# Attention of a gated cross-attention and expert layer: split products against whole fp32 operands

## The chip, the cores and the metric

The kernel is one program on one core of a Trainium2 chip. The metric is the device time of one execution in microseconds (us), the median of three runs. An execution takes about 2.16 ms.

## The reference, cut to what matters

The layer has two halves: a cross-attention from 32 batches of 256 tokens (256 features) to 77 context rows plus one null row, 16 heads of 64, and a mixture of 32 experts of which each token takes 8, with a shared expert. Each half is added to its input through a gate.

```python
q = split_heads(x @ Wq)                         # x: (32, 256, 256), layer-normalised
k, v = split(context @ Wkv)                     # context: (32, 77, 512)
k = concat(null_kv[0], k); v = concat(null_kv[1], v)      # 78 rows a head
attn = softmax(q * 64 ** -0.5 @ k.T)            # (32, 16, 256, 78)
out = layernorm((attn @ v) @ Wout)
x = x + tanh(g_xattn) * out
# then: router logits, top 8 of 32, weighted sum of the experts' gated MLPs, shared expert
x = x + tanh(g_ffn) * ffn(layernorm(x))
```

## The kernel before

The kernel has three stages. The context phase (`context_phase`, to about 242 us) multiplies the context by `Wkv` in four groups of eight batches and stores keys and values to DRAM. The attention phase (`attention_phase`) runs one step a batch, b from -2 to 33. The expert phase (`expert_phase`) works through 159 pages of 512 routed rows and 16 dense rounds; its first dense rounds run between the last attention steps.

**Split products.** A tile that enters a product is kept as two tiles of type fp32r, a high part and a low part. ACT copies a result out of PSUM into the high tile (`high`, L932), DVE subtracts that from PSUM into the low tile (`low`, L1170), and `split_product` (L138) issues three products: high by high, low by high, high by low.

**One attention step.** PE follows a written order, `RING` (L92): X transposes the normalised tokens of the batch after, N2 those of an earlier batch for the router, Oa and Ob are the output projection of the batch before, T0a to T3b transpose the probabilities, L and R are the router's logits and ranks, Q0 to Q3 the queries of the next batch, PV0a to PV1b the products of probabilities and values. Every name has one of four PSUM banks (`BANK`, L94), and PE waits in `free` (L1303) until the bank's holder before has been read. The scores of a batch are four units (two token tiles, two halves of the heads), made by `similarity` (L1282) at the start of a step (units 0 and 1) and after Oa (2 and 3): per unit four pairs of heads, each a product of 156 columns, two heads side by side in a key tile `kT` whose other halves are zero. So a step has 16 x 3 = 48 score products.

DVE takes the negated maximum of a unit (L1026), ACT the exponentials (L921), DVE normalises (L1031). The normalised probabilities are written in two pieces: 64 columns of each head (`main`), and the remaining 14 of eight heads together (`rest`, 112 columns). PE transposes `main` two heads at a time (T0a, T1a, T2a, T3a: four transposes each) and `rest` in T1b and T3b (two each): 20 transposes a step. A value product takes two heads' `main` rows, with the values on a block diagonal (`v_main`), and adds a second product with the `rest` rows (`v_rest`); 8 pairs x 2 x 3 = 48 products of 256 columns a step.

**Order on the other engines.** ACT and DVE run through `EVICTED` in PE's order, with the exponentials, normalisations, maxima and router operations hung in behind certain names (L983 to L1010, L1241 to L1268). POOL computes the two inverse deviations of a step (`make_rstd`, L833) and issues 16 indirect scatters a step of 128 rows to their pages from step 3 on (`scatter`, L844); the scatters and the statistics stand in one order (L857 to L906), and the first scatter of a step waits until the page fills of the steps before have landed. DVE's second statistics of a step stand behind the low part of T3b (L1250), and POOL's second `make_rstd` waits for them. Router product R uses Ob's bank, which `centre` (L1057) frees, and `centre` waits for POOL's first `make_rstd`.

**SP's queue.** One queue (L737 to L794) issues, step by step: the tokens two batches ahead, page fills, the values of the next batch (18 loads: two of `v_main`, eight heads of `v_rest` with two parts each), the keys of the next batch (four loads, L671), and stores. At the start come 16 loads that place the null value row (L760).

In the context phase ACT evicts each product into a high tile (L364 to L378), DVE subtracts the low part (L429 to L438), and both parts are stored; a high and a low key array and a values array of twice the width lie in DRAM.

## Time and profile before

| what | value |
|---|---|
| median of 3 runs | 2156.69 us (2154.57 to 2160.22) |
| span of the profiled execution | 2156.4 us |
| PE busy | 2034.8 us (94%) |
| DVE busy | 1768.4 us (82%) |
| ACT busy | 1387.1 us (64%) |
| POOL busy | 1204.5 us (56%) |
| DMA packets, under 512 B of them | 442777, 204984 |

The page gives the profiled execution's span, from its first to its last instruction; it has no other time for that execution. Busy time counts an engine as busy while any record of it runs. PE's records overlap, so a PE that is busy is not a PE at its peak: distances between the starts of records tell its pace. In a row of the order in time the columns are start in us, length in us, engine, line, operation, output and inputs, form, and, in brackets, the idle time before it with what ended it; "x4" is four instructions merged. PEld is PE's weight load, SPq and POOLq are the issue of DMAs by those engines. Shares over the whole span mix the three stages, so windows by stage come first.

### The profile page before, as it was taken

To read this page: it belongs to the slowest core of one execution; us is meant where nothing else is said; L and a number is where in the kernel's file an instruction comes from. 1 tells how busy PE (TensorE), PEld (TensorE's weight loads), DVE (VectorE), ACT (ScalarE), POOL (GpSimd) and SP (SyncE) were. 2 spreads that over 40 slices of the span, in tenths; PEclk is the share of its full clock that TensorE was granted. 3 is DMA by queue.
4 is the path that set the end of the run, shared out by engine and by line. 5 is a ranking of instruction groups with operands and counts; after the bars stand their busy time and mean duration, and the time that the engine had idled before them with its cause. 6 is when DMAs were issued, how large, how long until landed. Compare 5 with 4: busy or idle time off the path is not lost. (4 is left out here: it accounts for less than half of the span.)

```text
span 2156.4 us, 43812 instructions
## 1 busy us (share of the span) xinstructions
PE 2034.8 (94%) x14306; PEld 1884.7 (87%) x14306; DVE 1768.4 (82%) x4190; ACT 1387.1 (64%) x4030; POOL 1204.5 (56%) x1324
## 2 busy tenths in 40 slices
PE   7999689999999999999997889999999999999995
PEld 7888589999999999999997778988988888888884
DVE  4544258899999999999997766668999999999996
ACT  3322357677777777777774347777777777777771
POOL 0000202777777777777777600006777777777775
PEclk9999889999999999999998899999999999999997
DMA  9876489988888888788886999999999999999997
GB/s 275 280 242 216 140 240 297 304 262 249 246 252 252 252 249 250 248 249 246 248 259 224 298 360 286 287 285 365 403 403 402 397 397 395 391 392 399 393 366 280
DMA packets 442777, 645.86 MB, mean 300 GB/s; under 512 B 204984, under 2 KB 317337, under 8 KB 440089
## 3 DMA queue, kind: packets, MB, share of 16 engines
q1 hardware_dynamic: 393400, 508.79, 71.0%
q0 software_dynamic: 49152, 134.28, 17.2%
q8 instruction: 116, 1.90, 0.4%
q14 instruction: 109, 0.88, 0.1%
HBM read 325.18 MB, written 317.72 MB: 298 GB/s over the span
## 5 line engine op out<-in xcount | busy, mean ns | idle before, releaser
L1710 POOL DMA_INDIRECT parts<-results_dram,kept_index x512 | 516.1, 1008 | 382.7 <-DMA results_dram<-y 219.0
L848 POOL DMA_INDIRECT pages_dram<-rows,kept_index x512 | 509.4, 995 | 167.0 <-issue 139.1
L927 ACT ACTIVATE exps<-sim,minus_max 128x78 f32<-128x78 f32 x1024 | 320.8, 365 | 50.5 <-DVE minus_max L1028 49.9
L927 ACT ACTIVATION_READ_ACCUMULATOR exps<-sim,minus_max 128x1 f32 x1024 | 252.3, 247 | 0.0
L1731 ACT ACTIVATE w_h<-w_raw 128x768 fp32r<-128x768 f32 x159 | 134.0, 843 | 149.7 <-DMA w_raw<-in_experts 149.7
L1819 DVE SCALAR_TENSOR_TENSOR parts<-parts,kept_weight 128x256 f32<-128x256 f32 x448 | 213.6, 477 | 1.8 <-DMA parts<-dense_dram 0.7
L1916 PE MATMUL xps<-ident,xin 128*128 128x128 f32 x1272 | 167.0, 275 | 18.1 <-DVE wq_l L1781 7.9
L1793 DVE TENSOR_TENSOR w_l<-w_raw,w_h 128x768 fp32r<-128x768 f32 x159 | 151.7, 954 | 38.6 <-ACT w_h L1731 38.4
L140 PE MATMUL yps<-w_h,hid_h 128*128 128x256 f32 x636 | 180.0, 283 | 0.7 <-DVE hid_l L1876 0.7
L142 PE MATMUL yps<-w_l,hid_h 128*128 128x256 f32 x636 | 178.7, 281 | 0.0
L141 PE MATMUL yps<-w_h,hid_l 128*128 128x256 f32 x636 | 178.2, 280 | 0.0
L1738 ACT ACTIVATE y<-yps 128x512 f32<-128x512 f32 x318 | 171.8, 597 | 1.5 <-PE yps L142 1.5
L1916 PEld LDWEIGHTS xps<-ident,xin 128*128 128x128 f32 x1272 | 141.0, 141 | 26.1 <-issue 24.2
L140 PE MATMUL ring<-xnT_h,wq_h 128*128 128x256 f32 x512 | 157.7, 308 | 2.0 <-DVE xnT_l L1175 1.4
L1762 ACT ACTIVATE hid_h<-up_ps 128x512 fp32r<-128x512 f32 x175 | 103.4, 591 | 85.5 <-DVE up_ps L1870 85.0
L1781 DVE TENSOR_TENSOR wq_l<-xps,wq_h 128x512 fp32r<-128x512 f32 x212 | 143.0, 686 | 18.5 <-ACT wq_h L1725 18.5
L140 PE MATMUL sim<-kT_h,qT_h 128*128 128x156 f32 x512 | 140.9, 275 | 11.9 <-issue 7.7
L1870 DVE SCALAR_TENSOR_TENSOR up_ps<-up_ps,w_raw,act_gate 128x512 f32<-128x512 f32 x159 | 120.0, 755 | 38.0 <-PE up_ps L142 36.6
L140 PE MATMUL ring<-wo_h,outT_h 128*128 128x256 f32 x512 | 148.7, 290 | 0.2 <-DVE outT_l L1175 0.2
L141 PE MATMUL ring<-xnT_h,wq_l 128*128 128x256 f32 x512 | 145.6, 284 | 0.0
L142 PE MATMUL ring<-xnT_l,wq_h 128*128 128x256 f32 x512 | 145.3, 284 | 0.0
L141 PE MATMUL ring<-wo_h,outT_l 128*128 128x256 f32 x512 | 143.5, 280 | 0.0
(270 smaller groups left out, 7206.5 us busy)
## 6 DMA issues: line engine op xcount, KB each, us to landing
xin<-pages_dram SPq DMA_DIRECT2D x159, 512.0 KB, 10.5
results_dram<-y SPq DMA_DIRECT2D x159, 512.0 KB, 9.6
w_raw<-in_experts SPq DMA_DIRECT2D x159, 385.0 KB, 9.5
pages_dram<-blank SPq DMA_DIRECT2D x108, 512.0 KB, 4.0
pages_dram<-blank SPq DMA_DIRECT2D x12, 1536.0 KB, 8.2
values_dram<-values SPq DMA_DIRECT2D x16, 1024.0 KB
v_main<-values_dram SPq DMA_DIRECT2D x64, 256.0 KB
keys_h_dram<-keys_h SPq DMA_DIRECT2D x16, 616.0 KB, 4.8
```

Source lines behind the costliest of these rows:

```text
L140: eng.matmul(out, left[0], right[0], start=start, stop=False)
L141: eng.matmul(out, left[1], right[0], start=False, stop=False)
L142: return eng.matmul(out, left[0], right[1], start=False, stop=stop)
L848: pool.indirect_dma_start(dram["pages"], bass.IndirectOffsetOnAxis(ap=kept_index[:, at:at + 1].bitcast(U32), axis=0), buffer(batch)[:, k / ...
L927: last = act.activation(exps[u % 2][:, h, :], scores(u)[:, h // 4, h % 4, :], ACT.Exp, bias=minus_max[u][:, h:h + 1], accum_out=row_sum[u] ...
L1710: pool.indirect_dma_start(parts[slot(batch, t)][:, k, :], None, done, bass.IndirectOffsetOnAxis(ap=kept_index[:, at:at + 1].bitcast(U32), ...
L1731: act.activation(w_split[s][0][:, :], w_raw[s][:, 0:EW], ACT.Copy).then_inc(w_hi, 1)
L1738: last = act.activation(y[s][:, q:q + 2, :], yps[:, q:q + 2, :], ACT.Copy)
L1781: dve.tensor_tensor(xT[m % XT][1][:, c, :], xps[:, c, :], xT[m % XT][0][:, c, :].bitcast(F32), ALU.subtract).then_inc(x_lo, 1)
L1793: dve.tensor_tensor(w_split[s][1][:, :], w_raw[s][:, 0:EW], w_split[s][0][:, :].bitcast(F32), ALU.subtract).then_inc(w_lo, 1)
L1819: dve.scalar_tensor_tensor(out=out, in0=part[:, k, :], scalar=kept.weight[:, at:at + 1], in1=part[:, TOPK, :], op0=ALU.mult, op1=ALU.add). ...
L1916: last = pe.transpose(xps[:, c, q * P:(q + 1) * P], xin[s][:, q, c * P:(c + 1) * P], ident[:, :])
```

## The change

Attention works on whole fp32 operands instead of split ones.

- *Scores.* `qT` and `kT` become single fp32 tiles; a pair of heads is one fp32 product of 156 columns, 16 a step instead of 48. The queries have no low part.
- *Transposes.* The probabilities of a head stay together, 78 columns; each head is transposed by itself, 32 transposes a step in eight names (T0a, T0b, ... T3b), and ACT evicts 78 partitions of 512 columns into one fp32 tile `pT`. There is no low part.
- *Values.* `v` is one tile of 78 rows by 16 heads by 64. A value product takes one head: 64 columns of weights, 256 columns of `pT`. The even head of a pair writes PSUM partitions 0 to 63, the odd one 64 to 127. 16 products a step instead of 48.
- *Waits.* Only X, N2 and the value results still have low parts (`SPLIT`); users of the others wait for ACT alone. The second statistics still stand behind T3b, whose low part is skipped. `RING` and `BANK` are rewritten: T0a and T0b, T1a and T1b, T2a and T2b, T3a and T3b are neighbours, and the banks go round in another order.
- *Context phase.* DVE alone copies keys and values out of PSUM, ACT does nothing for them; DVE waits for the stores. Keys and values are stored once, half the bytes.
- *DMA.* Per step one load of values instead of 18, two of keys instead of four. The null value row is loaded by two DMAs at the start of SP's queue instead of being split and placed by 16. POOL no longer clears value tiles.

```diff
...
-RING = ["X", "N2", "Oa", "T0a", "Ob", "T1a", "L", "Q0", "T1b", "Q1", "PV0a", "PV0b", "T2a", "R", "T3a", "Q2", "T3b", "Q3",
-        "PV1a", "PV1b"]
-BANK = {"X": 1, "N2": 2, "Oa": 3, "T0a": 0, "Ob": 3, "T1a": 1, "L": 2, "Q0": 0, "T1b": 1, "Q1": 2, "PV0a": 1, "PV0b": 0, "R": 3,
-        "T2a": 2, "T3a": 1, "Q2": 0, "T3b": 3, "Q3": 2, "PV1a": 1, "PV1b": 0}
+RING = ["X", "N2", "Oa", "T0a", "T0b", "Ob", "T1a", "T1b", "L", "Q0", "Q1", "PV0a", "PV0b", "T2a", "T2b", "R", "T3a", "T3b", "Q2",
+        "Q3", "PV1a", "PV1b"]
+BANK = {"X": 2, "N2": 0, "Oa": 3, "T0a": 1, "T0b": 2, "Ob": 3, "T1a": 0, "T1b": 1, "L": 2, "Q0": 0, "Q1": 1, "PV0a": 2, "PV0b": 0,
+        "T2a": 1, "T2b": 2, "R": 3, "T3a": 0, "T3b": 1, "Q2": 2, "Q3": 3, "PV1a": 0, "PV1b": 1}
 NBANK = 4
 EVICTED = [n for n in RING if n[0] not in "OLR"]
+SPLIT = [n for n in EVICTED if n in ("X", "N2") or n[0] == "P"]
...
-ROUTE_AFTER = {"T1a": ["logits", "top", "mask"], "PV0b": ["placed"], "Q3": ["opened", "page", "moved", "slot"],
+ROUTE_AFTER = {"T1b": ["logits", "top", "mask"], "PV0b": ["placed"], "Q3": ["opened", "page", "moved", "slot"],
...
-                        for out, tile in zip(keys_out, keys[unit % KSLOTS]):
-                            sp.dma_start(out[:, g * CG + i * CBATCHES:g * CG + (i + 1) * CBATCHES, first:first + KPART * M],
-                                         tile[:, :, :, :].rearrange("p b q m -> p b (q m)").bitcast(F32)).then_inc(keys_stored[unit % KSLOTS], 16)
+                        sp.dma_start(keys_out[:, g * CG + i * CBATCHES:g * CG + (i + 1) * CBATCHES, first:first + KPART * M],
+                                     keys[unit % KSLOTS][:, :, :, :].rearrange("p b q m -> p b (q m)")).then_inc(keys_stored[unit % KSLOTS], 16)
...
-                    act.wait_ge(full, at(PRODUCTS, name, g))
-                    ps = bank(name)
-                    if name[0] == "K":
-                        pair, unit = int(name[2]), key_unit(name, g)
-                        if pair % KPART == 0 and unit >= KSLOTS:
-                            act.wait_ge(keys_stored[unit % KSLOTS], 32 * (unit // KSLOTS))
-                        last = act.activation(keys[unit % KSLOTS][0][:, :, pair % KPART, :],
-                                              ps[:, 0:CCOLS].rearrange("p (b m) -> p b m", m=M), ACT.Copy)
-                    else:
-                        t, half, unit = int(name[1]), int(name[2]), value_unit(name, g)
-                        if half == 0 and unit >= VSLOTS:
-                            act.wait_ge(values_stored[unit % VSLOTS], 16 * (unit // VSLOTS))
-                        last = act.activation(values[unit % VSLOTS][0:size(t), 0, half * 512:(half + 1) * 512],
-                                              ps[0:size(t), :], ACT.Copy)
-                    signal(last)
+                    skip()
...
+                    dve.wait_ge(full, at(PRODUCTS, name, g))
                     ps = bank(name)
                     if name[0] == "K":
-                        high, low = (tile[:, :, int(name[2]) % KPART, :] for tile in keys[key_unit(name, g) % KSLOTS])
-                        last = dve.tensor_tensor(low, ps[:, 0:CCOLS].rearrange("p (b m) -> p b m", m=M), high.bitcast(F32),
-                                                 ALU.subtract)
+                        pair, unit = int(name[2]), key_unit(name, g)
+                        if pair % KPART == 0 and unit >= KSLOTS:
+                            dve.wait_ge(keys_stored[unit % KSLOTS], 16 * (unit // KSLOTS))
+                        last = dve.tensor_copy(keys[unit % KSLOTS][:, :, pair % KPART, :], ps[:, 0:CCOLS].rearrange("p (b m) -> p b m", m=M))
                     else:
-                        t, half = int(name[1]), int(name[2])
-                        high, low = (values[value_unit(name, g) % VSLOTS][0:size(t), part, half * 512:(half + 1) * 512] for part in range(2))
-                        last = dve.tensor_tensor(low, ps[0:size(t), :], high.bitcast(F32), ALU.subtract)
+                        t, half, unit = int(name[1]), int(name[2]), value_unit(name, g)
+                        if half == 0 and unit >= VSLOTS:
+                            dve.wait_ge(values_stored[unit % VSLOTS], 16 * (unit // VSLOTS))
+                        last = dve.tensor_copy(values[unit % VSLOTS][0:size(t), half * 512:(half + 1) * 512], ps[0:size(t), :])
...
-    kT = [sb(f"kT_{s}", [P, PAIRS, 2 * J], F32R) for s in "hl"]
-    v_main = [sb(f"v_main{i}", [P, 2, PAIRS, P], F32R) for i in range(2)]
-    v_rest = [sb(f"v_rest{i}", [P, 2, 2, HP, P], F32R) for i in range(2)]
-    qT = [sb(f"qT_{s}", [P, PAIRS, N], F32R) for s in "hl"]
+    kT = sb("kT", [P, PAIRS, 2 * J])
+    v = [sb(f"v{i}", [J, HEADS, DH]) for i in range(2)]
+    qT = sb("qT", [P, PAIRS, N])
     exps = [sb(f"exps{i}", [P, PAIRS, J]) for i in range(2)]
-    probs = [sb(f"probs{i}", [P, PAIRS * J]) for i in range(2)]
-    pT = [sb(f"pT_{s}", [P, HP + 1, N], F32R) for s in "hl"]
+    probs = [sb(f"probs{i}", [P, PAIRS, J]) for i in range(2)]
+    pT = sb("pT", [J, PAIRS, N])
...
-        if name in ("T1b", "T3b"):
-            return ps[0:PAIRS * REST, 0:N], [t[0:PAIRS * REST, HP, :] for t in pT]
         if name[0] == "T":
-            tt = int(name[1]) % 2
-            return ps[:, :].rearrange("p (h n) -> p h n", h=4), [t[:, 0:HP, tt * P:(tt + 1) * P] for t in pT]
+            tt, h = int(name[1]) % 2, HP * "ab".index(name[2])
+            return ps[0:J, :].rearrange("p (h n) -> p h n", h=HP), [pT[:, h:h + HP, tt * P:(tt + 1) * P]]
         if name[0] == "Q":
             q = 2 * int(name[1])
-            return by_two, [t[:, q:q + 2, :] for t in qT]
+            return by_two, [qT[:, q:q + 2, :]]
...
-            for part, name in zip(kT, ("keys_h", "keys_l")):
-                of_batch = dram[name][batch].rearrange("p (q m) -> p q m", m=M)
-                for half, col in halves:
-                    sp.dma_start(part[half, :, col:col + M].bitcast(F32), of_batch[half, :, :]).then_inc(keys_loaded, 16)
+            of_batch = dram["keys"][batch].rearrange("p (q m) -> p q m", m=M)
+            for half, col in halves:
+                sp.dma_start(kT[half, :, col:col + M], of_batch[half, :, :]).then_inc(keys_loaded, 16)
 
         def load_values(batch):
 
-            of_batch = dram["values"][batch * M:(batch + 1) * M, :]
-            by_pair = of_batch.rearrange("m (a s d) -> m a s d", s=2, d=DH)
-            by_head = of_batch.rearrange("m (a h d) -> m a h d", h=PAIRS, d=DH)
-            main = v_main[batch % 2][:, :, :, :].rearrange("p s q d -> p (s q) d")
-            rest = v_rest[batch % 2][:, :, :, :, :].rearrange("p s f q d -> p (s f) q d")
-            for s in range(2):
-                sp.dma_start(main[s * DH:(s + 1) * DH, :, s * DH:(s + 1) * DH].bitcast(F32),
-                             by_pair[0:DH, :, s, :]).then_inc(values_loaded[batch % 2], 16)
-            for head in range(PAIRS):
-                col = head % 2 * DH
-                sp.dma_start(rest[head * REST:(head + 1) * REST - 1, :, head // 2, col:col + DH].bitcast(F32),
-                             by_head[DH:M, :, head, :]).then_inc(values_loaded[batch % 2], 16)
+            sp.dma_start(v[batch % 2][0:M, :, :].rearrange("m h d -> m (h d)"),
+                         dram["values"][batch * M:(batch + 1) * M, :]).then_inc(values_loaded[batch % 2], 16)
...
-        sp.dma_start(null_v[:, :], dram["null_kv"][1:2, :]).then_inc(null_loaded, 16)
+        for values in v:
+            sp.dma_start(values[M:J, :, :], dram["null_kv"][1:2, :].unsqueeze(1).broadcast_to([1, HEADS, DH])).then_inc(null_v_loaded, 16)
...
-                if b == -1:
-                    sp.wait_ge(zeroed, 1)
-                elif b >= 1:
+                if b >= 1:
...
-                if name == "T0a" and here:
+                if name == "T0b" and here:
                     exp(3, b, 0, PAIRS // 2)
-                if name == "T1a" and here:
+                if name == "T1b" and here:
...
-                dve.wait_ge(ring_full, nth(RING, "T1b" if before_u < 2 else "T3b", before_b))
-            e, inv = exps[u % 2], row_inv[u][:, :].unsqueeze(2)
-            main = probs[u % 2][:, 0:PAIRS * DH].rearrange("p (h j) -> p h j", j=DH)
-            rest = probs[u % 2][:, PAIRS * DH:PAIRS * J].rearrange("p (h j) -> p h j", j=REST)
-            dve.tensor_tensor(main, e[:, :, 0:DH], inv.broadcast_to([P, PAIRS, DH]), ALU.mult)
-            dve.tensor_tensor(rest, e[:, :, DH:J], inv.broadcast_to([P, PAIRS, REST]), ALU.mult).then_inc(probs_ready, 1)
+                dve.wait_ge(ring_full, nth(RING, f"T{before_u}b", before_b))
+            dve.tensor_tensor(probs[u % 2][:, :, :], exps[u % 2][:, :, :], row_inv[u][:, :].unsqueeze(2).broadcast_to([P, PAIRS, J]),
+                              ALU.mult).then_inc(probs_ready, 1)
...
-            if not runs(name, b):
+            if name not in SPLIT or not runs(name, b):
...
-                if name == "T1b" and here:
+                if name == "T1a" and here:
...
-            pe.wait_ge(ring_lo, nth(EVICTED, "Q3", b - 1))
-            pe.wait_ge(keys_loaded, 64 * (b + 1))
+            pe.wait_ge(ring_hi, nth(EVICTED, "Q3", b - 1))
+            pe.wait_ge(keys_loaded, 32 * (b + 1))
             if n == 0:
                 pe.wait_ge(keys_zeroed, 1)
-                pe.wait_ge(null_k_lo, 1)
+                pe.wait_ge(null_k_set, 1)
             if n >= 2:
                 pe.wait_ge(exp_done, n - 1)
             tt, half = u % 2, u // 2
             for i in range(HP):
                 pair = half * HP + i
-                last = split_product(pe, sim[u % 2][:, i // 2, (i % 2) * 2 * J:(i % 2 + 1) * 2 * J],
-                                     [t[:, pair, tt * P:(tt + 1) * P] for t in qT], [t[:, pair, :] for t in kT])
+                last = pe.matmul(sim[u % 2][:, i // 2, (i % 2) * 2 * J:(i % 2 + 1) * 2 * J], qT[:, pair, tt * P:(tt + 1) * P],
+                                 kT[:, pair, :], start=True, stop=True)
...
-                        pe.wait_ge(ring_lo, nth(EVICTED, held, at))
+                        pe.wait_ge(ring_lo if held in SPLIT else ring_hi, nth(EVICTED, held, at))
...
-            elif name in ("T1b", "T3b"):
-                first = int(name[1]) - 1
-                pe.wait_ge(probs_ready, UNITS * b + first + 2)
-                for tt in range(TT):
-                    last = pe.transpose(ps[0:PAIRS * REST, tt * P:(tt + 1) * P], probs[tt][:, PAIRS * DH:PAIRS * J], ident[:, :])
             elif name[0] == "T":
-                u = int(name[1])
+                u, first = int(name[1]), HP * "ab".index(name[2])
                 pe.wait_ge(probs_ready, UNITS * b + u + 1)
                 for i in range(HP):
-                    last = pe.transpose(ps[:, i * P:(i + 1) * P], probs[u % 2][:, i * P:(i + 1) * P], ident[:, :])
+                    last = pe.transpose(ps[0:J, i * P:(i + 1) * P], probs[u % 2][:, first + i, :], ident[:, :])
...
-                pe.wait_ge(values_loaded[par], 16 * (2 + PAIRS) * (h + 1))
+                pe.wait_ge(values_loaded[par], 16 * (h + 1))
                 if b == 0:
-                    pe.wait_ge(null_placed, 32 * PAIRS)
-                pairs = [2 * "ab".index(name[3]) + i for i in range(2)]
-                pe.wait_ge(ring_lo, nth(EVICTED, f"T{2 * half + 1}a", b))
-                for i, pair in enumerate(pairs):
-                    split_product(pe, ps[:, i * N:(i + 1) * N], [main_values(b, part, HP * half + pair) for part in range(2)],
-                                  [t[:, pair, :] for t in pT], start=i == 0, stop=False)
-                pe.wait_ge(ring_lo, nth(EVICTED, f"T{2 * half + 1}b", b))
-                for i, pair in enumerate(pairs):
-                    last = split_product(pe, ps[:, i * N:(i + 1) * N], [rest_values(b, part, half, pair) for part in range(2)],
-                                         [t[0:PAIRS * REST, HP, :] for t in pT], start=False, stop=i == 1)
+                    pe.wait_ge(null_v_loaded, 32)
+                pe.wait_ge(ring_hi, nth(EVICTED, f"T{2 * half + 1}b", b))
+                first = HP * "ab".index(name[3])
+                for i in range(2):
+                    for rows_of, _ in halves:
+                        head = first + 2 * i + (rows_of.start > 0)
+                        last = pe.matmul(ps[rows_of, i * N:(i + 1) * N], v[par][:, PAIRS * half + head, :], pT[:, head, :], start=True, stop=True)
...
```

## Rows read from the trace of the kernel before

**Rows 1.** Windows: length, busy (count) of PE, PEld, DVE, ACT, POOL; clock, DMA, GB/s

```profile
259.40:295.20 35.80, 24.86 (x168) 23.51 (x169) 16.48 (x33) 19.11 (x85) 0.00 (x0) 0.79 0.55 142
354.20:390.20 36.00, 30.21 (x234) 29.57 (x235) 28.30 (x77) 19.95 (x85) 17.67 (x21) 0.91 0.98 333
692.40:719.85 27.45, 27.32 (x235) 26.81 (x234) 25.97 (x80) 20.39 (x85) 20.62 (x24) 1.00 0.82 249
```

**Rows 2.** PE in time order: first score product of steps 1 and 31

```profile
295.23 0.47 PE L140 MATMUL sim<-kT_h,qT_h 128*128 128x156 f32 x1 [7.08 <-issue]
...
1132.19 0.24 PE L140 MATMUL sim<-kT_h,qT_h 128*128 128x156 f32 x1
```

**Rows 3.** PE in time order: transposes, then value and score products

```profile
701.32 0.61 PE L1343 MATMUL ring<-ident,probs 128*128 128x128 f32 x4
701.68 0.37 PE L140 MATMUL ring<-wo_h,outT_h 128*128 128x256 f32 x1
701.89 0.28 PE L141 MATMUL ring<-wo_h,outT_l 128*128 128x256 f32 x1
...
716.98 0.28 PE L140 MATMUL ring<-pT_h,v_main 128*128 128x256 f32 x1
...
719.85 0.24 PE L140 MATMUL sim<-kT_h,qT_h 128*128 128x156 f32 x1
719.92 0.28 PE L141 MATMUL sim<-kT_h,qT_l 128*128 128x156 f32 x1
...
720.48 0.28 PE L140 MATMUL sim<-kT_h,qT_h 128*128 128x156 f32 x1
```

**Rows 4.** POOL in time order, one step: scatters, wait for the statistics

```profile
692.54 1.07 POOL L848 DMA_INDIRECT pages_dram<-rows,kept_index  x1 [0.29 <-issue]
...
718.19 0.19 POOL L835 TENSOR_TENSOR var_eps<-mean_var,eps_col 128x2 f32<-128x2 f32 x1 [1.91 <-DVE mean_var L1053]
...
719.99 1.07 POOL L848 DMA_INDIRECT pages_dram<-rows,kept_index  x1 [0.30 <-issue]
```

**Rows 5.** Waits (us, times, longest): steps in 540 to 977, then context phase

```profile
POOL var_eps L835 <- DVE mean_var L1053: 30.5, 16, 1.9
...
ACT values L376 <- DMA values_dram<-values: 17.8, 5, 9.9
```

**Rows 6.** SP's queue in time order, during step 0

```profile
261.38 9.84 SPq L763 DMA_DIRECT2D v_rest<-null_rows  x16
...
285.96 2.02 SPq L674 DMA_DIRECT2D kT_h<-keys_h_dram  x2
```

**Rows 7.** POOL in time order, first scatter of step 3

```profile
365.48 1.24 POOL L848 DMA_INDIRECT pages_dram<-rows,kept_index  x1 [12.18 <-DMA pages_dram<-blank]
```

**Rows 8.** PE in time order, products of 512 columns in the expert phase

```profile
1319.72 0.39 PE L141 MATMUL gate_ps<-wq_h,w_l 128*128 128x512 f32 x1
...
1322.05 0.39 PE L142 MATMUL up_ps<-wq_l,w_h 128*128 128x512 f32 x1
```

**Rows 9.** Groups in 540:977.6: count, busy us, mean ns, idle before

```profile
L1175 DVE TENSOR_TENSOR pT_l<-ring,pT_h 128x512 fp32r<-128x512 f32 x64 | 44.0, 687 | 1.1
L1175 DVE TENSOR_TENSOR qT_l<-ring,qT_h 128x512 fp32r<-128x512 f32 x64 | 43.5, 679 | 4.0 <-ACT qT_h L939 4.0
L1175 DVE TENSOR_TENSOR outT_l<-ring,outT_h 128x512 fp32r<-128x512 f32 x64 | 42.1, 678 | 0.0
L939 ACT ACTIVATE pT_h<-ring 128x512 fp32r<-128x512 f32 x63 | 39.3, 625 | 7.4 <-PE ring L1343 7.4
L1069 DVE SCALAR_TENSOR_TENSOR x<-z,rstd,x 128x256 f32<-128x256 f32 x32 | 14.0, 478 | 0.0
L1061 DVE SCALAR_TENSOR_TENSOR z<-ring,mean_var,scale_row 128x256 f32<-128x256 f32 x32 | 13.9, 476 | 0.0
L1049 DVE BATCH_NORM_STATS2 stats<-x 128x6 f32<-128x256 f32 x32 | 11.9, 414 | 0.0
```

**Rows 10.** PE's weight loads in time order, one of a score product

```profile
720.19 0.19 PEld L141 LDWEIGHTS sim<-kT_h,qT_l 128*128 128x128 f32 x1
```

More of the change, by code:

```diff
@@ L186, in context_phase @@
     ctxT = [sb(f"ctxT_{s}", [P, CC, CROWS], F32R) for s in "hl"]
-    keys = [[sb(f"keys{i}_{s}", [P, CBATCHES, KPART, M], F32R) for s in "hl"] for i in range(KSLOTS)]
-    values = [sb(f"values{i}", [P, 2, INNER], F32R) for i in range(VSLOTS)]
+    keys = [sb(f"keys{i}", [P, CBATCHES, KPART, M]) for i in range(KSLOTS)]
+    values = [sb(f"values{i}", [P, INNER]) for i in range(VSLOTS)]
     banks = [ctx.enter_context(nc.psum_tensor(f"bank{i}", [P, 512], F32)) for i in range(CBANK)]
@@ L223, in staged @@
         return s.rearrange("p (c n) -> p c n", c=shape[1]) if len(shape) == 3 else s
-    keys_out = [dram[f"keys_{s}"].rearrange("b p f -> p b f") for s in "hl"]
+    keys_out = dram["keys"].rearrange("b p f -> p b f")
     def size(t):
@@ L628, in null_keys @@
         return [null_k[half, 0:1].broadcast_to([DH, PAIRS]) for half, _ in halves]
-    def main_values(batch, part, pair):
-        return v_main[batch % 2][:, part, pair, :]
-    def rest_values(batch, part, half, pair):
-        return v_rest[batch % 2][0:PAIRS * REST, part, half, pair, :]
     def buffer(batch):
@@ L805, in gpsimd @@
         pool.wait_ge(made, 3)
-        for part in kT:
-            for (half, _), (_, col) in zip(halves, reversed(halves)):
-                last = pool.memset(part[half, :, col:col + J].bitcast(F32), 0.0)
+        for (half, _), (_, col) in zip(halves, reversed(halves)):
+            last = pool.memset(kT[half, :, col:col + J], 0.0)
         last.then_inc(keys_zeroed, 1)
@@ L967, in step @@
             if b == -2:
-                act.wait_ge(null_loaded, 16)
-                act.activation(null_rows[:, 0, :, :], null_v[:, :].unsqueeze(1).broadcast_to([1, 2, DH]), ACT.Copy).then_inc(null_hi, 1)
                 act.wait_ge(null_k_loaded, 32)
                 for (half, col), null in zip(halves, null_keys()):
-                    last = act.activation(kT[0][half, :, col + M], null, ACT.Copy)
-                last.then_inc(null_k_hi, 1)
+                    last = act.activation(kT[half, :, col + M], null, ACT.Copy)
+                last.then_inc(null_k_set, 1)
             if b == 0:
```

40 lines of the change are left out of this document (8 added, 32 removed).

## The prediction, made before the changed kernel was run

> **What bounds the kernel now.** I read the windows by stage first [rows 1]. From 390 us on the attention steps repeat, and in one of them PE is busy 27.32 of 27.45 us at full granted clock (1.00), DVE 25.97, ACT 20.39 and POOL 20.62. The step starts, in PE's order of time, give the period: from step 16 to step 31, (1132.19 - 719.85) / 15 = 27.49 us [rows 2, 3]. So PE sets the step, and what a step costs is the sum of the distances between starts of its products, not the length of their records: records of 0.28 us start 0.11 to 0.12 us apart [rows 3].
>
> The next thing to read is who comes second. POOL looks three quarters busy, but its order of time [rows 4] shows scatters of about 1.0 us, sixteen a step, with 0.30 us of issue before each, and in a whole step (692.54 to 719.99, 27.45 us) it waits for another engine only once: 1.91 us for DVE's second statistics. In 16 steps that wait is 30.5 us [rows 5], 1.91 each. Hence POOL by itself needs 27.45 - 1.91 = 25.54 us a step. A faster PE meets that floor after less than 2 us.
>
> The four first steps are longer: 259.4 to 390.2, 130.8 us for four [rows 1]. Step 0 ends in a stall, 7.08 us before step 1's first score product [rows 2], and the granted clock of step 0's window is 0.79 (part of it at 1.2 GHz, the lower of the two levels). SP's order shows why: 16 loads of the null row take 9.84 us, values behind them, and the keys of step 1 are only issued at 285.96 [rows 6]. Step 3 is long because POOL's first scatter waits 12.18 us for the page fills [rows 7], which stand in the same SP queue.
>
> **The change, part by part**, against the profiled span of 2156.4 us (the median of the three runs, 2156.69, is 0.3 above it; I treat them as one).
>
> *Score products.* 48 of 156 columns become 16 whole fp32 ones. Before: 719.92 to 720.48 is five distances, 0.112 us each [rows 3], so 48 x 0.112 = 5.38 us a step. The trace has no whole fp32 product except transposes. Its floor is one of the present ones, 0.112; its ceiling follows from the kernel's own split, which treats an operand as a high and a low part: a product of two whole operands is at most four such products with a load each, 0.448. Between them lies four passes in which the loads stay hidden: 512-column products start 0.233 us apart (ten distances from 1319.72 to 1322.05, [rows 8]), 0.455 ns a column, so 4 x 156 columns take 0.284 us. I take that, because in rows 3 and 8 a load never shows where the columns take longer than it. 16 x 0.284 = 4.54: -0.84 us. The Trainium skill, "FP8 and Floating Point Precision", TensorE Precision Notes, puts a true fp32 product at four passes; by it the sum is this middle value, and no run here shows it yet.
>
> *Value products.* Before, 24 in 716.98 to 719.85, 0.1196 each [rows 3], 48 x 0.1196 = 5.74 us. After, 16 products of 256 columns and 64 output rows, alternately in the two column halves: 4 x 256 x 0.455 ns = 0.466 us each, 7.45 us one after another, 3.73 us if the halves run side by side. Floor 0.06 each (one pass, side by side), ceiling 4 x 0.1196 = 0.478. I take side by side, since the two products share neither weights, columns nor output rows: -2.01 us. No row of before shows two products in different halves, so this is the weakest step.
>
> *Entering and leaving the half-width form.* Twice a step, four edges. The nearest row is the change from transposes to products: 701.68 to 701.89, 0.21 instead of 0.11 [rows 3], 0.10 an edge, +0.40 us. If PE empties at each edge, a record less its distance is added, 0.28 - 0.12 = 0.16 more, and the sum below ends some 18 us higher. The Trainium skill, "TensorEngine Tiling (Array Packing)", Key Properties, states such a drain; rows 3 show a smaller cost for a change of kind of another sort, so they decide neither way.
>
> *Transposes.* 20 a step become 32. Four take 0.36 us from their first start to the next group's (701.32 to 701.68, [rows 3]), 0.09 each. With 78 columns to load instead of 128, 0.055 to 0.09; at 0.07, 32 x 0.07 - 20 x 0.09 = +0.44 us (-0.04 to +1.08).
>
> *PE's step* is then 27.49 - 0.84 - 2.01 + 0.40 + 0.44 = 25.48 us, a hair under POOL's 25.54. The ends of all bounds together put PE between 19 and 33 us; below 25.5 the floor is POOL's.
>
> *DVE and ACT.* DVE loses the low parts of the transposes (44.0 us in 15.9 steps, and a shorter tile beside) and of the queries (43.5), over 5.5 us a step [rows 9], and one of two products in each normalisation: from 26 to about 20 us busy. ACT evicts eight transposed tiles instead of six, at most 8 x 0.625 against 4 x 0.625 and two shorter ones [rows 9], under +2.5 us, to less than 23 of 25.5. Neither binds. Transposes and queries are free after ACT alone, so PE's waits on them end earlier.
>
> *Where POOL's wait goes.* It waits because the second statistics stand in DVE's order behind the low part of T3b. That low part is gone, so from rstd to the statistics there remain centre (2 x 0.476), two low parts of outT (2 x 0.678), the residual (2 x 0.478) and the statistics (2 x 0.414), 4.1 us [rows 9], and some 0.6 for small ones, under the 4 x 1.3 = 5.2 us that POOL spends on four scatters meanwhile. A new wait comes in: T2b uses the bank of PV0a, whose low part stands on DVE behind centre, which waits for POOL's rstd; behind T2b on PE stand R, T3, Q2 and PV1, and ACT and DVE wait for those. With PE and POOL within 0.1 us of each other and handing over once a step, I add 0.2: 25.75 us. That is 1.74 us a step over 28 steps (4 to 31): -48 us.
>
> *The start.* The 16 null loads and 17 of 18 value loads a step leave SP, so the keys of step 1 no longer come late, and POOL's memsets of the value tiles go. Two null-row loads now stand ahead of the null key on SP, which ACT and then PE wait for, under 1 us. Steps 0 to 3 I put at 30, 26, 25.5 and 31.5 (the fills are still there, so half of that wait stays): 113 against 130.8, -18 us; -8 to -25.
>
> *Context phase.* PE bounds it. Evictions go from ACT and DVE to DVE alone, the same count on DVE. DVE, no longer ACT, waits for the stores (17.8 us in five waits, the longest 9.9, [rows 5]), with the context splits and statistics queued behind; the stores are half as large, so I cost it at nothing, up to 10 us if one wait reaches PE.
>
> *The end.* After step 31 only scatters that run at POOL's pace and the untouched expert phase are left. Nothing is taken or added.
>
> Sum: 2156.4 - 48 - 18 = 2090 us.
>
> **The rivals.**
> (1) *Halves in turn (slower).* If the second half starts only when the first is done, value products cost 7.45 us and PE's step is 29.2 us: +1.7 x 28 = +48, the start gives back 3: 2201 us. PE's step is 21.75 + 16p for a price p of one value product, with the other terms as above; over p = 0.38 the kernel is slower, at 0.236 POOL takes over. With dearer or cheaper score products and transposes the case spans 2155 to 2210. For it: nothing in the trace shows two products side by side; against it: loads already run beside products, and the operands are separate.
> (2) *The step stays near its old length.* Either the four passes of a product are issued in order and only its last one overlaps the next half (six passes for a pair instead of four: 5.59 us, PE 27.3), or POOL goes on waiting 1.91 us because DVE's chain is not under 5.2. Then mainly the start is gained: 2138 to 2142, spanning 2112 to 2150.
> (3) *Loads that show.* Each pass with a load of its own that is not hidden, both products at their ceilings: +1.79 + 1.91 + 0.84 on PE, 32.0 us a step: about 2290, from 2210 up. Against it: a load of 0.19 us [rows 10] goes with each of the products that start 0.112 apart, all in the same rows, so loads overlap products now. The Trainium skill, "TensorE: Matmul & The Clock Gate", Part 3, lets a load overlap a running product only in another row group, which the two halves are not; the trace contradicts that for the present products.
>
> **How the numbers follow.** Forecast 0.50 (2073 to 2112: start -25 to -8, step 25.5 to 26.2), rival 2 0.17, rival 1 0.23, rival 3 0.10. A measurement of this kernel tells 0.3% from no change, 6.5 us: faster is under 2150, slower over 2163. Faster: 0.50 + 0.17 + 0.01 = 0.68; the same 0.04, all of rival 1; slower 0.18 + 0.10 = 0.28. The range 2073 to 2198 leaves out rival 3, 0.07 of rival 1 and 0.03 below; the forecast's own range is 2073 to 2112.
>
> **What will show it.** In the profile after: 156-column products 0.28 us of PE apart, and value products in pairs that start together or 0.23 us apart on average (0.47: rival 1); POOL busy or issuing through the whole step with var_eps's wait gone; PE with a small wait for DVE at T2b or R each step; no stall before step 1; DVE near 20 us a step. The prediction is wrong if PE is still without any idle time at a step over 27 us, if POOL's step is not 25.5, or if steps 0 to 3 keep their 130 us.

## The result, and the profile after

The changed kernel takes 2177.45 us (median of 4 runs, 2176.34 to 2183.12) where the kernel before takes 2155.63: 1.0100 times as long, with a 95% interval of 1.0084 to 1.0117. The forecast was 2090. The change makes the kernel 1% slower, and the sign of the forecast was wrong. The profiled execution has a span of 2176.0 us, 19.6 more than before.

The starts of the steps say where this lies. Step 0's first score product comes at 254.01, 5.4 us earlier than before [rows 1]. Steps 0 to 3 take 111.4 us (254.01 to 365.38) against 130.8, 19.4 less. The 27 steps 4 to 30 take 786.7 us (365.38 to 1152.07), 29.14 each, against 27.48 [rows 1, 2]: 44.6 more. From step 31 to the end it is 1023.9 against 1024.2. The start gave about what was forecast, the end nothing, and all the loss is in the repeated step.

The windows of the profile after answer to [rows 1]. They are step 0, step 3, then steps 16 and 17. The columns are length, busy time (count) of PE, PEld, DVE, ACT and POOL, granted clock, DMA share, GB/s.

```profile
254.01:283.03 29.02, 24.32 (x148) 20.10 (x148) 9.72 (x18) 20.82 (x87) 0.00 (x0) 0.76 0.71 257
337.32:365.38 28.06, 26.16 (x216) 23.41 (x214) 19.94 (x63) 22.03 (x88) 19.11 (x22) 1.00 0.84 294
714.46:742.74 28.28, 26.05 (x215) 23.30 (x213) 20.43 (x64) 22.03 (x88) 21.98 (x25) 1.00 0.64 220
742.74:772.65 29.91, 27.68 (x216) 24.94 (x214) 20.44 (x64) 22.02 (x88) 21.92 (x25) 0.94 0.62 208
755.00:758.20 3.20, 3.20 (x17) 3.20 (x16) 0.00 (x0) 1.41 (x9) 2.73 (x3) 0.50 0.80 221
```

Two things are new. PE is busy for 26.05 of 28.28 us in step 16, where before it was busy for 27.32 of 27.45 us; DVE fell to 20.4 us, as forecast, and ACT rose to 22.0, so no engine is full any more. And there are two lengths of step, 28.3 and 29.9 us: of the 27 steps, 14 have the longer one. The longer step holds a stretch at a granted clock of 0.50 (the lower of the two levels, 1.2 GHz), which is the last row.

PE's order of time in step 17 shows both (columns as in [rows 3]):

```profile
751.26 0.60 PE L1276 MATMUL ring<-ident,probs 128*78 128x128 f32 x4
753.93 0.63 PE L1276 MATMUL ring<-ident,probs 128*78 128x128 f32 x4 [2.06 <-DVE xnT_l L1121]
754.32 0.37 PE L140 MATMUL ring<-wo_h,outT_h 128*128 128x256 f32 x1
...
754.75 0.28 PE L140 MATMUL ring<-wo_h,outT_h 128*128 128x256 f32 x1
754.87 0.35 PE L141 MATMUL ring<-wo_h,outT_l 128*128 128x256 f32 x1
755.01 0.42 PE L142 MATMUL ring<-wo_l,outT_h 128*128 128x256 f32 x1
755.23 0.42 PE L140 MATMUL ring<-wo_h,outT_h 128*128 128x256 f32 x1
...
758.51 0.28 PE L141 MATMUL ring<-wo_h,outT_l 128*128 128x256 f32 x1
```

The first row is T0a, the second T0b. Between them PE stands for 2.06 us and waits for DVE's `xnT_l`. That is the low part of X, and X holds bank 2, which the new `BANK` gives to T0b next. This wait comes in every step from 0 to 30: 0.64, 1.08, 1.19 and 1.73 us in the first four, and from step 4 on 2.06 us but for one of 2.42. Behind it come Ob's products, first 0.12 us apart, then from 755.01 to 758.2 us 0.21 apart.

DVE's order of time in the same step shows why `xnT_l` is late:

```profile
744.11 0.81 DVE L977 TENSOR_REDUCE minus_max<-sim 128x8 f32<-128x624 f32 x1 [0.28 <-PE sim L1232]
...
746.67 0.67 DVE L1138 TENSOR_REDUCE kept_weight<-of_key 128x16 f32<-128x512 f32 x1
747.45 0.69 DVE L1128 TENSOR_TENSOR of_key<-key,top_key 128x512 f32<-128x512 f32 x1
...
748.28 0.81 DVE L988 TENSOR_TENSOR probs<-exps,row_inv 128x624 f32<-128x624 f32 x1
...
750.62 0.79 DVE L977 TENSOR_REDUCE minus_max<-sim 128x8 f32<-128x624 f32 x1
...
751.75 0.81 DVE L988 TENSOR_TENSOR probs<-exps,row_inv 128x624 f32<-128x624 f32 x1
752.47 0.80 DVE L977 TENSOR_REDUCE minus_max<-sim 128x8 f32<-128x624 f32 x1
753.19 0.68 DVE L1121 TENSOR_TENSOR xnT_l<-ring,xnT_h 128x512 fp32r<-128x512 f32 x1
753.79 0.68 DVE L1121 TENSOR_TENSOR x2T_l<-ring,x2T_h 128x512 fp32r<-128x512 f32 x1
758.95 0.76 DVE L995 BATCH_NORM_STATS2 stats<-ring 128x6 f32<-128x256 f32 x2 [4.48 <-PE ring L142]
```

From its second row on, up to 754.4 us, DVE waits for no other engine: three maxima, two normalisations and the router's work stand ahead of `xnT_l` in its written order. Behind it DVE is idle for 4.48 us, because PE was held up and Ob is late. An engine with 8 us to spare in a step is late at the one place where PE needs it.

The waits in 540 to 977 us (sum, times, longest) answer to [rows 5]:

```profile
DVE stats L995 <- PE ring L142: 57.5, 15, 4.5
POOL var_eps L786 <- DVE mean_var L999: 35.8, 24, 2.7
PE ring L1276 <- DVE xnT_l L1121: 31.3, 15, 2.4
```

The chain goes on: DVE's statistics wait for Ob, POOL's `var_eps` waits for them. POOL's wait, which I expected to go, grew from 1.91 to 35.8 / 15 = 2.4 us a step: some 1.3 us in a step of 28.3 us, and two waits of 0.4 and 2.7 us in one of 29.9.

### The profile page after: what moved, and what is told of

Read it like the earlier page. It is cut to its first block and busy times, and to the rows that moved or that the text cites. A ratio compares the mean times of both kernels' runs of the same rounds, so it can differ in the third digit from the quotient of the medians.

```text
span 2176.0 us, 41763 instructions
## 1 busy us (share of the span) xinstructions
PE 2008.4 (92%) x13666; PEld 1784.6 (82%) x13666; DVE 1587.1 (73%) x3739; ACT 1390.5 (64%) x3989; POOL 1233.9 (57%) x1318
## 5 line engine op out<-in xcount | busy, mean ns | idle before, releaser
L799 POOL DMA_INDIRECT pages_dram<-rows,kept_index x512 | 538.8, 1052 | 160.2 <-issue 130.3
L878 ACT ACTIVATION_READ_ACCUMULATOR exps<-sim,minus_max 128x1 f32 x1024 | 233.3, 228 | 0.0
L1276 PE MATMUL ring<-ident,probs 128*78 128x128 f32 x1024 | 150.2, 281 | 65.1 <-DVE xnT_l L1121 60.7
L890 ACT ACTIVATE pT<-ring 78x512 f32<-78x512 f32 x256 | 145.3, 594 | 86.8 <-PE ring L1276 80.2
L1276 PEld LDWEIGHTS ring<-ident,probs 128*78 128x78 f32 x1024 | 106.4, 120 | 95.5 <-DVE xnT_l L1121 68.9
L1121 DVE TENSOR_TENSOR outT_l<-ring,outT_h 128x512 fp32r<-128x512 f32 x128 | 87.9, 687 | 121.8 <-ACT outT_h L890 118.6
L1846 PEld LDWEIGHTS xps<-ident,xin 128*128 128x128 f32 x1272 | 140.9, 141 | 27.1 <-issue 25.1
L140 PE MATMUL ring<-wo_h,outT_h 128*128 128x256 f32 x512 | 158.7, 310 | 3.5 <-DVE outT_l L1121 0.5
L1232 PE MATMUL sim<-kT,qT 128*128 128x156 f32 x1024 | 156.1, 303 | 4.4 <-ACT exps L878 3.7
L1232 PEld LDWEIGHTS sim<-kT,qT 128*128 128x128 f32 x1024 | 140.1, 191 | 21.1 <-issue 17.7
```

The source lines that it names most:

```text
L140: eng.matmul(out, left[0], right[0], start=start, stop=False)
L799: pool.indirect_dma_start(dram["pages"], bass.IndirectOffsetOnAxis(ap=kept_index[:, at:at + 1].bitcast(U32), axis=0), buffer(batch)[:, k / ...
L878: last = act.activation(exps[u % 2][:, h, :], scores(u)[:, h // 4, h % 4, :], ACT.Exp, bias=minus_max[u][:, h:h + 1], accum_out=row_sum[u] ...
L1232: last = pe.matmul(sim[u % 2][:, i // 2, (i % 2) * 2 * J:(i % 2 + 1) * 2 * J], qT[:, pair, tt * P:(tt + 1) * P], kT[:, pair, :], start=Tru ...
L1276: last = pe.transpose(ps[0:J, i * P:(i + 1) * P], probs[u % 2][:, first + i, :], ident[:, :])
L1846: last = pe.transpose(xps[:, c, q * P:(q + 1) * P], xin[s][:, q, c * P:(c + 1) * P], ident[:, :])
```

## The experiments: whose wait it is

Theory: the bank of T0b costs 2.06 us a step, and the idle PE brings the half clock. Rival: DVE or POOL sets the step anyhow, and PE's idle time only shows it. The first two runs move one name each.

**T0b behind Ob.** Ob's products need nothing of X, and take 2.8 us.

```diff
-RING = ["X", "N2", "Oa", "T0a", "T0b", "Ob", "T1a", ...
+RING = ["X", "N2", "Oa", "T0a", "Ob", "T0b", "T1a", ...
```

> The written order of the PE is changed by one name: T0b stands behind Ob instead of ahead of it. Theory (bank wait): in every step from 3 to 31 PE stands 2.06 us at T0b, because its bank is held by X until DVE has made xnT_l; Ob's 24 products need nothing of that and take 2.8 us, so they cover it. The wait goes (29 x 2.06 = 60 us), and the stretches at half the granted clock that follow it in some steps go too (12 of 1.6 us, 20 us): a step of about 26 us and 2096 us in all, 2085 to 2115. Rival (other engine): DVE, late by 2 us at xnT_l, or POOL sets the step anyway, and the wait turns up elsewhere: 2150 to 2177.

Measured: 2115.34 us, 0.9806 of the kernel before (0.9785 to 0.9828). The mean of steps 4 to 30 is 26.95 us, and no stretch at half clock is left in them. PE's order of time:

```profile
722.56 0.60 PE L1276 MATMUL ring<-ident,probs 128*78 128x128 f32 x4
722.92 0.36 PE L140 MATMUL ring<-wo_h,outT_h 128*128 128x256 f32 x1
...
725.83 1.47 PE L1276 MATMUL ring<-ident,probs 128*78 128x128 f32 x12
...
728.81 0.38 PE L140 MATMUL ring<-xnT_h,wq_h 128*128 128x256 f32 x1 [0.63 <-ACT pT L890]
```

T0b and both names of T1 follow Ob at 725.83 without a wait. The time lies at the upper end of what was expected, since a smaller wait came in, 0.63 us at Q0, whose bank ACT has not yet emptied. One exchange of two names in PE's order is worth 62 us and turns the loss into a gain of 2%.

**X's low part earlier.** PE's order stays; DVE makes `xnT_l` ahead of one maximum.

```diff
                 normalise(1, b)
+                low("X", b)
                 maximum(3, b)
...
             for name in EVICTED if b >= -1 else ():
-                low(name, b)
+                if name != "X":
+                    low(name, b)
```

> DVE makes xnT_l ahead of the maximum of unit 3 instead of behind it; PE's order is as in the changed kernel. Theory (bank wait): the wait at T0b shrinks by the 0.72 us that the maximum takes, to about 1.35 us, in 29 steps: 21 us less, 2156 us; if the stretches at half clock need an idle PE of some 2 us they go as well, 2136 us. Rival (the wait is for something else than X's bank): unchanged at 2177.

Measured: 2130.25 us, 0.9874 (0.9852 to 0.9896). PE's order of time:

```profile
701.38 0.60 PE L1280 MATMUL ring<-ident,probs 128*78 128x128 f32 x4
703.33 0.63 PE L1280 MATMUL ring<-ident,probs 128*78 128x128 f32 x4 [1.35 <-DVE xnT_l L1121]
```

The wait shrank by 0.71 us, as long as a maximum, so it is DVE's order that sets it. The step is 27.60 us, 1.54 shorter: 0.71 of wait and 0.83 that the half clock had cost. The rest of the 47 us is in steps 0 to 3, 5.3 us shorter. With 1.35 us of idle time a step the granted clock stays at 1.00 in steps 4 to 30.

**The wait filled.** Eighteen extra products of the form of Ob's are issued between T0a and T0b.

```diff
+                if name == "T0a" and 1 <= b < B:
+                    for i in range(18):
+                        pe.matmul(bank("Ob", b)[:, D:2 * D], outT[0][:, i % PAIRS, P:2 * P], wo[0][:, i % PAIRS, :], ...)
```

> As the changed kernel, with 18 more products of 256 columns between T0a and T0b, into the columns that Ob overwrites afterwards, 18 x 0.115 = 2.07 us: as long as the wait. The result is that of the kernel; the work is extra. Theory (the idle PE lowers the clock): the wait is covered, PE is never idle, no stretch at 0.50 of the clock is left, every step takes 28.3 us: 27 x 0.85 = 23 us less, about 2154. Rival (the clock falls for a reason that the idle time does not make): unchanged at 2177. Rival (the wait is not fixed by DVE but follows PE): 2.07 us a step more, about 2237.

Measured: 2155.37 us, 0.9984 of the kernel before (0.9972 to 0.9996), 22 us less than the changed kernel although PE does 2.07 us more a step. Every step takes 28.3 us (mean 28.30). The window of one step (columns as above):

```profile
1004.00:1032.30 28.30, 28.13 (x233) 25.42 (x232) 20.43 (x64) 21.99 (x87) 22.05 (x25) 1.00 0.68 221
```

So the half clock follows from the idle time. Its price is 29.14 - 28.30 = 0.84 us a step, beside the 2.06 of the wait itself. Why it comes in 14 of the 27 steps and not in all stays open: the step with the longest wait, 2.42 us, has none.

## The experiments: what the products cost

**Both heads in one half.** The pair's two products go to the same partitions.

```diff
-last = pe.matmul(ps[rows_of, i * N:(i + 1) * N], v[par]...
+last = pe.matmul(ps[0:DH, i * N:(i + 1) * N], v[par]...
```

> Both heads of a pair write the same PSUM partitions 0 to 63, so the second product overwrites the first and half of the attention's output is left out; everything else is as in the changed kernel. Theory (the halves run side by side): one product is 0.235 us apart from the next in the changed kernel because two run at once; in one half each takes 0.466 us, 16 x 0.23 = 3.7 us more a step, about 2295 in all. Rival (a product costs 0.235 us by itself, wherever it writes): unchanged at 2177.

Measured: 2282.32 us. PE's order of time; a product shows as two records, so x16 are the eight products of two names:

```profile
788.91 3.67 PE L1293 MATMUL ring<-pT,v 78*64 78x256 f32 x16
792.51 0.31 PE L1276 MATMUL ring<-ident,probs 128*78 128x128 f32 x1
```

Eight products take 3.60 us, 0.45 each. In the changed kernel eight take 1.88 us, 0.235 each (763.44 to 765.32):

```profile
763.23 0.28 PE L142 MATMUL ring<-xnT_l,wq_h 128*128 128x256 f32 x1
763.44 1.95 PE L1293 MATMUL ring<-pT,v 78*64 78x256 f32 x16
765.32 0.41 PE L1276 MATMUL ring<-ident,probs 128*78 128x128 f32 x2
```

But here each product also writes the place its neighbour wrote, which might hold it up. The next run takes that away.

**One half, two places.** Base is the kernel with T0b behind Ob.

```diff
+last = pe.matmul(ps[0:DH, (rows_of.start > 0) * N:((rows_of.start > 0) + 1) * N], v[par]...
```

> As the kernel with T0b behind Ob, and all value products write partitions 0 to 63: the even head of a pair columns 0 to 255, the odd head columns 256 to 511, the second pair of a name over the first. Half of the attention's output is overwritten. No product writes where its neighbour just wrote, unlike in the run with one half and one place, where neighbours took 0.45 us each. Theory (two products overlap only in different halves): 0.45 us each again, 3.4 us more a step, about 2207 in all. Rival (what kept them apart was that both wrote the same place): 0.235 us each, 2115.

Measured: 2223.38 us, a step of 30.20 against 26.95. Eight products again take 3.60 us (737.97 to 741.57):

```profile
737.97 3.67 PE L1293 MATMUL ring<-pT,v 78*64 78x256 f32 x16
741.57 0.40 PE L1232 MATMUL sim<-kT,qT 128*128 128x156 f32 x1
```

So it is the half, not the place: two products run at once if, and here only if, they stand in different halves. The single records, which the rows above merge, show it directly. In the changed kernel they start two by two, 0.007 us apart, and a new pair comes every 0.216 us (763.704 and 763.711, 763.920 and 763.927). In one half they start one by one, every 0.216 us (789.174, 789.390).

**Evens, then odds.** Does the order within a name matter?

```diff
-for i in range(2):
-    for rows_of, _ in halves:
+for rows_of, _ in halves:
+    for i in range(2):
```

> As the kernel with T0b behind Ob, but in each name the two value products of the even heads come first and then those of the odd heads, so that neighbours in PE's order are in the same half twice in four. Theory (two neighbours overlap if they are in different halves, and each takes 0.45 us by itself): eight products take five slots of 0.45 us instead of four, 0.9 us more a step, about 2140. Rival (order does not matter): 2115. Rival (only neatly alternating products overlap at all): about 2205.

Measured: 2113.65 us, step 26.97, eight products in 1.93 us. My theory of neighbours falls: two and two cost 0.05 us more for eight products than one and one. Here too the single records start two by two, 0.01 us apart (814.268 and 814.280, 814.483 and 814.496). By the runs in one half such a pair must be of different halves, so an even and an odd product run at once although PE's order has both evens first.

## The experiments: what comes next

With T0b behind Ob a step takes 26.95 us: PE's 26.3 and a wait of 0.63 us at Q0, while POOL waits for 0.26 us. The last four runs ask which of them is the next bound.

**Exponentials behind T0a.**

```diff
-                if name == "T0b" and here:
+                if name == "T0a" and here:
                     exp(3, b, 0, PAIRS // 2)
```

> As the kernel with T0b behind Ob (2115 us, a step of 26.95 us), and ACT makes the first half of unit 3's exponentials behind the eviction of T0a instead of T0b. In that kernel PE waits 0.64 us a step at Q0, for ACT's eviction of T1a, which stands behind these exponentials, and POOL waits 0.26 us a step only. Theory (POOL's floor): PE's wait goes, its work is 26.95 - 0.64 = 26.3 us, but POOL needs 26.95 - 0.26 = 26.7: a step of 26.7 and some 7 us less, 2108. Rival (PE alone sets the step): 26.3, 28 x 0.64 = 18 us less, 2097. Rival (the wait turns up at the next product): 2115.

Measured: 2119.01 us, 0.9836 (0.9823 to 0.9849), a step of 27.10: nothing gained. PE's wait moved to T2 (0.57 us a step) and L (0.28), and `var_eps` no longer waits. The group of POOL's scatters in 540 to 977 us (count, busy us, mean ns, idle before), then two waits of that stretch:

```profile
L799 POOL DMA_INDIRECT pages_dram<-rows,kept_index x259 | 280.0, 1081 | 75.1 <-issue 65.7 <-DVE weight L1112 4.6 <-DVE kept_index L1088 4.6
```

```profile
DVE z L1007 <- POOL rstd L788: 31.5, 17, 1.9
PE ring L1276 <- DVE outT_l L1121: 9.1, 16, 0.6
```

POOL is the bound: `centre` waits for its `rstd`, the low part of outT behind it is late, and PE waits for that. Its floor is not the 26.7 us that I expected, because the scatters themselves changed: 1.081 us on average, 0.992 before. POOL's order of time shows them one by one, 0.96 us or about 1.5:

```profile
720.46 0.96 POOL L799 DMA_INDIRECT pages_dram<-rows,kept_index  x1 [0.30 <-issue]
721.73 1.57 POOL L799 DMA_INDIRECT pages_dram<-rows,kept_index  x1 [0.30 <-DVE weight L1112]
```

All 47 scatters over 1.15 us in 560 to 976 us run beside DVE's product `probs<-exps,row_inv`, which the change made one operation of 624 columns instead of two of 512 and 112. Not every scatter beside it is long, but no other scatter takes over 1.07 us. In the kernel before, with two pieces, 15 scatters of that stretch are over 1.15 us. Sixteen scatters at 0.089 us more are 1.42 us, and 25.54 + 1.42 = 26.96 is nearly the step.

**Exponentials behind T0a, and two pieces.**

```diff
+            for cols in (slice(0, DH), slice(DH, J)):
+                last = dve.tensor_tensor(probs[u % 2][:, :, cols], exps[u % 2][:, :, cols], ..., ALU.mult)
```

> As the kernel with the exponentials behind T0a, and DVE writes the normalised probabilities in two pieces (64 and 14 columns of each head), as the kernel before the change did, instead of one of 624. In the changed kernels POOL's scatters are longer on average (1.05 us against 0.99), the long ones beside that product. Theory (the one long product holds up scatters, and POOL sets the step): the scatters come back to 0.99, POOL's floor to 25.6, and PE's 26.3 sets the step: 2097. Rival (the length of the scatters has another cause): as without the pieces, about 2108.

Measured: 2107.18 us (six runs, 2103.46 to 2134.42), 0.980 (0.9759 to 0.984), a step of 26.67. The same group and waits:

```profile
L799 POOL DMA_INDIRECT pages_dram<-rows,kept_index x263 | 265.7, 1010 | 76.2 <-issue 66.1 <-DVE weight L1114 4.9 <-DVE kept_index L1090 4.6
```

```profile
POOL of_key L806 <- DVE minus_max L977: 12.1, 16, 0.8
PE ring L1308 <- ACT pT L890: 5.9, 16, 0.4
```

The scatters are almost back, at 1.010 us, and POOL waits 0.76 us a step again, so its floor is 25.9 us. That is the theory's cause, but its 2097 is missed by 10 us: PE's 26.3 and a wait of 0.37 us at L make the step.

**Two pieces alone**, without the exponentials' move:

> As the kernel with T0b behind Ob, with the normalised probabilities written in two pieces; the exponentials stay behind T0b, so PE's wait of 0.64 us at Q0 stays. Theory (PE and ACT set this kernel's step, POOL has 0.26 us to spare): the scatters shorten, POOL waits longer, the time stays at 2115. Rival (POOL sets this step already): 2105 to 2110.

Measured: 2115.84 us, 0.9826 (0.9811 to 0.9841), step 26.95 as without the pieces, though the scatters fell to 1.012 us. PE's 0.63 us at Q0 is unchanged. A floor that isn't touched is worth nothing when lowered.

**Three exponentials and five** on the kernel with both, to free L's bank earlier:

```diff
-                    exp(3, b, 0, PAIRS // 2)
+                    exp(3, b, 0, 3)
```

> As the kernel with the exponentials behind T0a and the probabilities in two pieces (2107 us, a step of 26.67), with three of unit 3's exponentials behind T0a and five behind T1b instead of four and four. There PE waits 0.39 us a step at L for ACT's eviction of T0b, which stands behind the fourth of them (0.30 us apart). Theory (that wait is all that keeps PE from its 26.3 us): 0.3 us a step less, 8 us in all, 2099. Rival (POOL or DVE sets the step by now): 2107.

Measured: 2106.85 us, 0.9768 (0.9744 to 0.9791), step 26.75. L's wait went, and 0.46 us came instead between T2a and T2b, behind `outT_l`, `centre` and POOL's `rstd`. The rival holds.

```profile
700.26 0.64 PE L1278 MATMUL ring<-ident,probs 128*78 128x128 f32 x4
701.36 0.63 PE L1278 MATMUL ring<-ident,probs 128*78 128x128 f32 x4 [0.46 <-DVE outT_l L1123]
```

These two kernels, about 2107 us, are the best of this study, 2% under the kernel before; PE, POOL and DVE hand over to each other there, and the longest waits of PE left in a step are 0.37 us in the one and 0.46 in the other.

## Why the prediction was wrong, point by point

PE's work is here a step less the time in which PE is idle, 28.28 - 2.06 us in step 16.

| a step of 4 to 30, us | forecast | measured |
|---|---|---|
| score products | 4.54 | 4.48 |
| value products | 3.73 | 3.76 |
| transposes and edges | 2.64 | 3.6 to 3.9 |
| PE's work in all | 25.48 | 26.2 |
| wait for a bank | 0.2 at T2b | 2.06 at T0b |
| half clock | 0 | 0.84 |
| step | 25.75 | 29.14 |

- **The step that failed** is "A new wait comes in: T2b uses the bank of PV0a". The mechanism was the right one, a bank whose holder has a low part, but I followed one name through the new order and not all. T0b uses the bank of X, with only N2, Oa and T0a between them, and at T2b no wait came in the changed kernel. PE waits at T0b instead, 2.06 us a step, as the runs that move T0b or `xnT_l` show. The wait that I forecast for T2b exists: it came, with 0.57 and 0.46 us, in two of the runs in which T0b no longer waits. In the paragraph before it I wrote that "PE's waits on them end earlier", which held for queries and transposes in the changed kernel but left X out, the tile that kept its low part. The price could have been read before the run. In the trace before, DVE's order of time in the step of [rows 3] has:

```profile
703.11 0.68 DVE L1175 TENSOR_TENSOR xnT_l<-ring,xnT_h 128x512 fp32r<-128x512 f32 x1
703.71 0.68 DVE L1175 TENSOR_TENSOR x2T_l<-ring,x2T_h 128x512 fp32r<-128x512 f32 x1
```

  PE is done with T0a and begins Ob at 701.68 [rows 3]; `xnT_l` is done at about 703.8. A product between T0a and Ob that needs X's bank would wait some 2 us. Before, none stood there: T1a took X's bank, after Ob.
- **The half clock** was not in the forecast: in the repeated step before, where PE was hardly ever idle, the granted clock was 1.00. It makes the 2.06 us cost 2.9. Not every new wait on PE has this price: those of 0.37 to 1.35 us in the runs above had none.
- **PE's work** came out 0.7 us higher than I put it. The transposes are 1.0 us or more dearer; some 0.3 came back in the queries, which transposes no longer interrupt. I took 0.07 us for one of 78 columns, between 0.055 and 0.09. T0a's four take 0.36 us as before, 0.09 each, and eight take 0.79 to 0.83 us, 0.10 each (766.96 to 767.79): fewer columns in the weights do not make a transpose shorter than the 0.09 of [rows 3]. The true sum lay outside my bounds.

```profile
766.96 1.07 PE L1276 MATMUL ring<-ident,probs 128*78 128x128 f32 x8
767.79 0.36 PE L140 MATMUL ring<-xnT_h,wq_h 128*128 128x256 f32 x1
```

- **Edges.** The step to value products costs 0.21 - 0.12 = 0.09 us (763.23 to 763.44). Leaving them for T2's transposes costs 0.25 (eight in 1.08 us instead of 0.83), leaving them for score products nothing. That is 0.43 a step, forecast 0.40. The Trainium skill, "TensorEngine Tiling (Array Packing)", Key Properties, says that a change of tiling mode drains the engine. These rows bear that out in part only: two of the three kinds of edge have a price, and a small one, and the third has none.
- **Score and value products** were right to 0.06 us a step: eight score products take 2.23 us (742.74 to 744.97), 0.28 each, as reckoned from four passes whose loads do not show, and the halves run side by side. That also refutes rival 3.

```profile
742.74 2.39 PE L1232 MATMUL sim<-kT,qT 128*128 128x156 f32 x16
744.97 0.60 PE L1271 MATMUL ring<-ident,xn 128*128 128x128 f32 x4
```

  Rival 1 is refuted by the runs in one half: its price of 0.466 us for a product by itself was measured as 0.45, but only where both write one half. That 2177 us lies in rival 1's span (2155 to 2210) is chance; its mechanism is not there.
- **POOL's floor** of 25.54 us held only for scatters of 0.99 us. With the one long product on DVE it is 26.7 to 27.1, with two pieces 25.9. So with the one long product 25.75 was out of reach, even without the bank wait.
- **POOL's wait** was to vanish, and grew to 2.4 us, since it hangs on Ob by way of DVE. My chain from rstd to the statistics, 4.1 us, also lacked a term: between centre and the low parts DVE waits 1.16 us in step 16 for ACT's `outT_h`, which waits for the value products. Where Ob comes in time POOL's wait for these statistics is 0.26 us or none.

```profile
735.36 1.48 DVE L1121 TENSOR_TENSOR outT_l<-ring,outT_h 128x512 fp32r<-128x512 f32 x2 [1.16 <-ACT outT_h L890]
```

- **The start** came out right as a sum, in part by luck: 111.4 us for steps 0 to 3, forecast 113, with no stall ahead of step 1. But the steps took 29.0, 26.8, 27.5 and 28.1 us where I had 30, 26, 25.5 and 31.5. In step 3 POOL's first scatter no longer waited for page fills; it waited 5.33 us for DVE's `kept_index`. The context phase gave 5.4 us that I had put at nothing. The end gave nothing, as forecast.

## What to carry to other kernels

When an order of work and its buffers are rewritten, walk every name: who held its buffer before, what frees it, and at what time the trace before shows that done, counted from the place where the new user will stand. A tile that drops its second reader frees its buffer early, but the tiles that keep theirs are then the slow ones in the ring, and neighbours in the new order meet them sooner. Leave work that does not need that buffer between the two, as Ob did here.

## What the runs showed of the hardware

- An idle PE can cost more than its length. In 14 of 27 steps an idle time of 2.06 us was followed, 0.5 to 1.4 us after work began again, by about 3.4 us at a granted clock of 0.50; in the other 13, with waits as long, it stayed at 1.00, as it did in steps 4 to 30 with 1.35 us of idle time a step, or none.
- POOL's indirect scatters grow from 0.96 to as much as 1.57 us beside a DVE product of two fp32 operands of 624 columns (from 0.99 us on average to between 1.05 and 1.08), and two pieces bring the average back to 1.01 us. The Trainium skill, "SBUF — State Buffer", Who interferes with whom, says that a tensor_tensor with both inputs in SBUF contends with an instruction of GpSimd (POOL) that reads SBUF, and infers that making descriptors is not held up by it. These scatters do take longer beside it; whether it is a read or the making of descriptors that is held up, no run tells.
- Two fp32 products of 64 output rows run at once when they stand in different column halves (0.235 us each instead of 0.45), whether they alternate or come two and two.
